# A DLRM tower on one Trainium2 core: when GpSimd issues a tile's gathers, and the order of the gram fills

## What is computed

```python
e = jnp.stack([tbl_f[ids[:, f]] for f in range(26)], axis=1)
sd = jnp.einsum('bfd,bd->bf', e, dense)
ss = jnp.einsum('bfd,bgd->bfg', e, e)          # upper triangle: 325 pairs
h = jnp.concatenate([dense, sd, pairs, dense], axis=1)
h = jnp.maximum(h @ W_top1 + b_top1, 0.0)      # 607 -> 512
h = jnp.maximum(h @ W_top2 + b_top2, 0.0)      # 512 -> 256
y = h @ W_top3                                 # 256 -> 1
```

## Time and profile before

| | before |
|---|---|
| timed runs, median of 3 | 369.42 us |
| profiled execution: its span, the only time of its own that it gives | 543.7 us |
| TensorE, mean granted clock | 0.836 |
| TensorE matmul / weight load busy | 392.0 / 342.7 us |
| VectorE / ScalarE / GpSimd busy | 233.2 / 186.9 / 253.7 us |
| VectorE, mean of a pack (L346); of a turning's transpose (L356) | 1.217; 1.830 us |
| DMA | 26.84 MB, mean 49 GB/s |

### The profile page before, as it was taken

The page is one execution under the profiler, slowest core; times in us unless marked ns, Lnnn a source line. Parts: engine busy times, 40 slices in busy tenths (PEclk is TensorE's granted clock), DMA queues, the critical chain, the costliest instruction groups (busy, mean ns, idle before and its releaser), DMA issues.

```text
span 543.7 us, 13728 instructions
## 1 busy us (share of the span) xinstructions
PE 392.0 (72%) x6224; PEld 342.7 (63%) x6224; DVE 233.2 (43%) x324; ACT 186.9 (34%) x283; POOL 253.7 (47%) x273
## 2 busy tenths in 40 slices
PE   5631776283986829876896959967795956969987
PEld 3520775272875718766685938857684934859876
DVE  6310887271461523635353533716454432555202
ACT  0110773231442323422324324513434313344453
POOL 6775627265263742627265363626465371552000
PEclk9955798595897958989797868979798885989999
DMA  8725105011020110201011011211112010110000
GB/s 229 204 54 128 30 20 190 26 41 43 12 59 26 46 39 17 59 21 53 23 41 53 24 43 28 58 27 45 35 41 54 20 51 17 40 49 22 2 4 2
DMA packets 11755, 26.84 MB, mean 49 GB/s; under 512 B 4652, under 2 KB 5804, under 8 KB 11570
## 3 DMA queue, kind: packets, MB, share of 16 engines
q0 software_dynamic: 8512, 17.45, 12.3%
q1 hardware_dynamic: 3186, 8.52, 5.5%
HBM read 25.95 MB, written 0.01 MB: 48 GB/s over the span
## 4 chain that ended last, share of the span: by engine, by line
PE 58%; another core or an unknown queue 24%; issue 10%; ACT 8%
PE sum_bank L592 22%; PE vec_bank L619 9%; PE work L644 8%; PE work L653 6%; PE vec_bank L605 5%; ACT vecT L426 4%; PE work L640 3%; ACT vecT L418 2%; PE id_bank L566 1%; PE work L633 1%; PE work L729 1%; PE work L659 0%; ACT parts L395 0%; ACT late L442 0%
## 5 line engine op out<-in xcount | busy, mean ns | idle before, releaser
L311 POOL DMA_INDIRECT rows<-in_tbl,ids_all x266 | 252.9, 951 | 245.6 <-PE vec_bank L619 143.8
L346 DVE TENSOR_TENSOR onehot<-id_bank,row_f 125x1024 fp32r<-125x1024 f32 x150 | 177.0, 1217 | 256.4 <-remote 133.7
L592 PE MATMUL sum_bank<-onehot,parts 125*128 125x256 f32 x1152 | 187.8, 306 | 54.3 <-issue 34.5
L592 PEld LDWEIGHTS sum_bank<-onehot,parts 125*128 125x128 f32 x1152 | 164.5, 204 | 67.4 <-issue 57.9
L426 ACT COPY vecT<-vec_bank 128x512 f32<-128x512 f32 (+1 forms) x74 | 83.2, 1128 | 82.1 <-remote 66.0
L418 ACT COPY vecT<-sum_bank 128x256 f32<-128x256 f32 x75 | 52.5, 700 | 118.0 <-remote 76.4
L619 PE MATMUL vec_bank<-vecT 128*26 128x26 f32 x4096 | 51.8, 200 | 45.8 <-issue 29.8
L619 PEld LDWEIGHTS vec_bank<-vecT 128*26 128x26 f32 x4096 | 45.0, 113 | 58.3 <-issue 52.5
L644 PE MATMUL work<-late,w_all 126*128 126x256 f32 (+1 forms) x192 | 51.5, 410 | 14.5 <-ACT late L442 14.5
L450 ACT ACTIVATE late<-work,w_all 128x256 f32<-128x256 f32 (+1 forms) x50 | 22.8, 458 | 95.5 <-remote 38.4
L605 PE MATMUL vec_bank<-ident,rows 128*128 128x128 f32 x266 | 45.8, 286 | 12.7 <-issue 10.9
(11 more groups left out here) (40 smaller groups left out, 106.3 us busy)
## 6 DMA issues: line engine op xcount, KB each, us to landing
rows<-in_tbl,ids_all POOLq DMA_INDIRECT x266
late<-in_tbl SPq DMA_DIRECT2D x7, 480.0 KB
w_all<-in_weights SPq DMA_DIRECT2D x1, 1571.0 KB
w_all<-in_tbl SPq DMA_DIRECT2D x3, 480.0 KB
xT<-in_dense_t SPq DMA_DIRECT2D x8, 128.0 KB
vecT<-in_ids_t SPq DMA_DIRECT2D x1, 256.0 KB, 2.9
late<-in_weights SPq DMA_DIRECT2D x1, 256.0 KB
ids_all<-in_ids SPq DMA_DIRECT2D x1, 208.0 KB, 2.3
```

Of the source, the lines that this page charges most:

```text
L311: nc.gpsimd.indirect_dma_start(rows[:, tile % TD, FG * j + n, :], None, tables[f], bass.IndirectOffsetOnAxis(ids_all[:, tile, f:f + 1], 0) ...
L346: nc.vector.tensor_tensor(onehot[:, use % RING, 0:width, :], bass.AP(got.tensor, got.offset, [got.ap[0], [0, width], [1, DS]]), bass.AP(nu ...
L592: last = nc.tensor.matmul(into_sum, parts[:, k, CH_AT[n] + c0 + c, :], hot, start=first and k == 0, stop=final and k == PARTS - 1)
```

## The change

On GpSimd, the wait before each group goes, and the wait for the gram of the tile two back stands before a tile's first group instead of its fourth. Before tile 1's first gather a wait for `pack_done` at 8 is added. On TensorE and ScalarE, the two gram halves of a tile (and their drains) are done one after the other, and the units and packs that stood between them follow. The order of the last two tiles is left as it is.

```diff
--- before.py
+++ after.py
@@ -19,7 +19,6 @@
 LOOKED_UP = ONEHOT + [SOMETIMES]
 TEN_STEPS = [3, 5, 7]
 LATE_SPLIT = 4
-GRAM_AHEAD_OF = 3
 SPLIT_AT_FIRST = len(LOOKED_UP) - LATE_SPLIT
 
 
@@ -96,6 +95,7 @@
     X_AFTER = 7
     LATE_LOW_AT = {2 * n: SPLIT_AT_FIRST + n for n in range(LATE_SPLIT)}
     SUM_AFTER = 5
+    TILE1_WAITS_FOR = 8
 
     STEP_USES = TD + M1 + M2 + 1
 
@@ -303,10 +303,10 @@
             pool.wait_ge(ids_loaded, 16)
             for tile in range(TILES):
                 for j in range(groups(tile)):
-                    if tile >= TD:
-                        pool.wait_ge(vec_filled, rows_at(same_rows(tile, j)[-1], j) + 1)
-                    if tile >= TD and j == GRAM_AHEAD_OF:
+                    if tile >= TD and j == 0:
                         pool.wait_ge(vec_filled, gram_at(tile - TD, 1) + 1)
+                    if tile == 1 and j == 0:
+                        pool.wait_ge(pack_done, TILE1_WAITS_FOR)
                     for n, f in enumerate(group(j)):
                         nc.gpsimd.indirect_dma_start(
                             rows[:, tile % TD, FG * j + n, :], None, tables[f],
@@ -487,6 +487,7 @@
                 d, t = tile // TD, tile % TD
                 for h in range(2):
                     drain_gram(tile, h)
+                for h in range(2):
                     if t == 0 and d:
                         drain_layer1(d - 1, 1 + h)
                     if t == 1 and d and h == 0:
```

## The result

The changed kernel takes 388.39 us (median of four runs, 387.43 to 391.17) against 369.22 us for the kernel before, beside which it ran: a ratio of 1.055, 95% interval 1.051 to 1.058. The forecast was no change, 369.4 us, in a range of 365.5 to 373.0; the measured time is 19 us above it, far outside the range.

The account below looks back on a forecast made before the run. The prediction took GpSimd's queue (359.6 us) as a little nearer to being the bound than TensorE's (353.2), side by side. From 369.4 us, adding 0.3 and subtracting 0.3 gave no change, 369.4, in a range of 365.5 to 373.0.

Parts of the forecast that it names:

- part 3: TensorE's adjacent gram halves: same instructions, so 0 us; layer 3's wait on ScalarE 0 to 0.2, seven times, taken as 0.
- The clock rival: TensorE: two gram halves in a row lower the clock, a 1.2 us half takes up to 1.71; 384 us, chance 0.03.
- parts 1, 2 and 4: GpSimd: dropped group waits 0 us, gram gate at first group 0, tile 1's pack wait 0.3 cost against 0.3 won.
- Tile 1's wait for eight packs: GpSimd before tile 1's gathers: packs done at 24.6, GpSimd there at 24.67; 0.3 us taken, bounds 0 to 8.7.
- GpSimd's sum of 359.6 us: GpSimd's queue: 266 gathers at 1.25 us end at 335.8, about 2 to land, 21.8 from last transposes to end.
- TensorE's sum of 353.2 us: TensorE's queue: 73.6 us to the second step, 243.3 for six steps with layers, 36.3 for the tail.
- a gram half 1.2: Term of TensorE's queue sum: each gram half takes 1.2 us, start to start at full clock.
- The slower rival: GpSimd is the bound and the new wait at tile 1 or tile 2's gate stops it: 372.2 us, chance 0.27.
- The faster one: Part of the profile's stall is in timed runs, and breaking the first gather run saves 3 us: 366.4, chance 0.28.
- the recording's own load: Profile reading: TensorE's spread-out matmuls during back-to-back gathers come from recording; the profile holds about 174 us beyond timed runs.

Follow-up runs that it names:

- the disturbed profile: First profile of the kernel before, with no edit: the profiled execution spans 543.7 us, while its three timed runs have a median of 369.42 us.
- The run in which gathers bound the kernel: The changed kernel's adjacent gram halves, with every second sample's products left out: 362.43 us, ratio 0.982 to the kernel before.
- the second profile: The kernel before profiled once more, with no edit: span 367.6 us, time 369.36 us.
- few gathers: The kernel before, halves apart, with the gathers of tiles 4 to 15 and TensorE's waits for them left out: 357.56 us.
- the adjacent kernels: Kernels with a tile's gram halves in a row: the changed kernel 388.39 us, adjacency alone 391.76, adjacency without gathers of tiles 4 to 15 389.53.

## Why the prediction was wrong

- **"Same instructions, so 0 on TensorE"** (part 3). This is the step that failed, and it carries all 19 us. The adjacent halves cost 16.3 us of gram time and some us of clock behind the stands, because the second block of 256 instructions in a pair comes 0.8 to 2.0 us later than the matmuls want it. I had counted instructions and their durations, and not the rate at which they must arrive. A sign stood in the rows: the gram half at 510.52 in the disturbed profile's tail, and the one at 527.34, were broken by idle of 0.65 and 0.99 us with nothing to wait for, and I did not ask why.
- **The clock rival** (chance 0.03) had its place right, two halves in a row, and its mechanism only as a follower. The stand comes first, at full clock (the matmuls at 126.00), and the lower clock after it. No rival had the supply of instructions.
- **The gates** (parts 1, 2 and 4) cost 0, as said: 0.9999 with them alone. GpSimd's list of waits in that run has no gram in it. Tile 1's wait for eight packs was free as well: in that run the eighth pack ends at 22.7 us, and GpSimd comes at 26.98. The prediction had 24.6 and 24.67.
- **GpSimd's sum of 359.6 us** came out by luck. The run in which gathers bound the kernel spans 360.1, but its last rows are there at 341.8 instead of 337.8, since six gathers beside VectorE's subtractions took longer, and its work behind them is shorter, since half of the gram is left out.
- **TensorE's sum of 353.2 us** was 14.4 short of the second profile's 367.6, and so the prediction named the wrong engine as nearer to the bound. The term is "a gram half 1.2": the row at 394.80 is from a stretch in which GpSimd, in the disturbed execution, stood still. Beside gathers a half takes 1.7, and 28 halves by 0.5 are 14 us. With few gathers the span is 355.8, near the sum.
- **The slower rival** foresaw the right sign with the wrong mechanism, GpSimd's wait going to the end. In the changed kernel GpSimd does wait for grams, 7 times and 15.7 us, but because the grams come late: with the old waits and adjacent halves the loss is the same. To read a slower result as GpSimd's bound, as the prediction proposed, would have misled. **The faster one** supposed that stalls of the earlier trace rows were in the timed runs. The second profile has none.
- **The unread part of the disturbed profile** was taken for "the recording's own load". It isn't: fourteen other profiled executions lie within 4 us of their timed runs. That page should have been used for durations only where GpSimd was as busy as in a timed run, and it had few such stretches.

## What to carry to other kernels

Count instructions per microsecond as well as their durations. Where TensorE runs hundreds of very short matmuls, keep wide ones between the runs: here a block of 256 instructions came no more often than every 3.3 us, and a run of 512 short ones stood until the second block came. A profile whose span is far off the timed runs is to be taken again, and a duration is only good for a sum if its neighbours were as busy as they will be.

## What the runs showed of the hardware

- TensorE's instructions arrive in 16 KB packets on a DMA queue of their own, 49 for this kernel, never less than 3.28 us from start to start. A packet holds 256 instructions: the stands of the adjacent kernels lie three times 256 apart, within one instruction. Matmuls go on 1.2 to 1.7 us after a packet's end.
- Indirect gathers in flight stretch a run of 128 narrow matmuls from 1.2 to 1.7 us. They left packs of wide ones as they were: 1.03 us on average with gathers, 1.05 with few.
- In the second profile of the kernel before, six gathers between 17 and 36 us that met VectorE's subtractions (L325) took 1.67 us, the first, and 1.84, the other five; the rest took 0.94. They cost GpSimd some 5 us. What they cost the kernel, no run tells.
- Open: why a packet starts only 0.8 to 1.7 us after the border before it, how gathers stretch a half, and what disturbed the first profiled execution.
